# A stretch of products in a quantised feed-forward: twelve up units multiplied anew, down weights moved out of SBUF, gated units kept as magnitudes

## What is computed

```
def act_qdq(x):                      # 16 bits, one scale for the whole tensor
    scale = max(max(abs(x)) / 32767, 1e-12)
    return clip(round(x / scale), -32768, 32767) * scale

x    = act_qdq(layernorm(x1))
up   = act_qdq(x @ dequant(w_up).T)
gate = act_qdq(x @ dequant(w_gate).T)
sig  = clip(round(sigmoid(gate) * 65536), 0, 65535) / 65536
gate = act_qdq(gate * sig)
o    = act_qdq(gate * up)
out  = x1 + o @ dequant(w_down).T
```

## Time and profile before

| what | value |
|---|---|
| median of the runs | 2325.39 us |
| the profiled execution, whole / its span | 2322.58 us / 2320.7 us |
| mean granted TensorE clock | 0.948 |
| busy: PE, DVE, ACT, POOL | 88%, 72%, 60%, 25% |
| matmuls of gate and up stage | 620.83 to 1618.49 us |
| no matmul | 1618.49 to 1811.57 us |
| matmuls of the down stage | 1811.57 to 2307.9 us |

### The profile page before, as it was taken

One profiled execution on the slowest core, in us unless ns is written; L12 is line 12 of the kernel. 1 busy time (PEld: TensorE's weight loads), 2 busy tenths in 40 slices (PEclk: granted clock), 3 DMA queues, 4 the chain that ended last, 5 costly groups with the idle time before them and its releaser, 6 DMA issues.

```text
span 2320.7 us, 25770 instructions
## 1 busy us (share of the span) xinstructions
PE 2031.3 (88%) x9780; PEld 975.5 (42%) x9780; DVE 1678.2 (72%) x1385; ACT 1401.9 (60%) x1599; POOL 578.9 (25%) x600
## 2 busy tenths in 40 slices
PE   5899999998699999999999999998000799999998
PEld 2455555554344444444444444444000344444443
DVE  8799999999444443532699997999899644488641
ACT  4588888886322322322698995666899643467530
POOL 2587777776100000000112111222110000000000
PEclk9999999999799999999999999999555899999999
DMA  7689999997348647633899994787998755545641
GB/s 294 261 312 364 361 366 364 355 371 300 136 167 267 258 164 230 223 144 141 299 393 382 376 363 176 295 322 288 414 417 328 284 227 216 205 195 218 236 154 73
DMA packets 131163, 634.63 MB, mean 273 GB/s; under 512 B 12256, under 2 KB 12768, under 8 KB 91104
## 3 DMA queue, kind: packets, MB, share of 16 engines
q1 hardware_dynamic: 85888, 316.81, 37.3%
q0 software_dynamic: 45152, 316.16, 34.8%
HBM read 430.69 MB, written 202.24 MB: 273 GB/s over the span
## 4 chain that ended last, share of the span: by engine, by line
PE 64%; DVE 3%; issue 3%; ACT 2%; POOL 0%; DVEq 0%; ACTq 0%; POOLq 0%
PE fd_pp L1778 43%; PE fd_pp L1792 21%; ACT ff_ring L1721 1%; DVE ff_sig L1576 1%; DVE ff_h_parts L1560 1%; DVE ff_sq L1498 1%; ACT ff_sig L1708 0%; DVE ff_sq L1567 0%; DVE kept_gate L1569 0%; DVE ff_gin L1511 0%; DVE ff_hq L1550 0%; ACT ff_ring L1747 0%; ACT ff_sig L1737 0%; ACT ff_hq L1633 0%; DVE kept_o_peak L1576 0%
## 5 line engine op out<-in xcount | busy, mean ns | idle before, releaser
L1792 PE MATMUL fd_pp<-ff_down,kept_gate 128*128 128x512 f16 x1536 | 457.9, 380 | 193.1 <-DVE ff_up L1617 193.1
L1778 PE MATMUL fd_pp<-ff_h_parts,kept_gate 128*128 128x512 f16 x2304 | 500.4, 381 | 14.7 <-DVE ff_h_parts L1416 14.7
L1778 PE MATMUL fd_pp<-ff_h_parts,ff_up 128*128 128x512 f16 x2304 | 497.4, 379 | 0.0
L1640 ACT ACTIVATE ff_raw<-fd_pp 128x1024 f32<-128x1024 f32 x192 | 194.3, 1017 | 397.4 <-PE fd_pp L1778 397.4
L1778 PEld LDWEIGHTS fd_pp<-ff_h_parts,kept_gate 128*128 128x128 f16 x2304 | 226.1, 98 | 288.8 <-DVE ff_h_parts L1416 15.0
L1778 PEld LDWEIGHTS fd_pp<-ff_h_parts,ff_up 128*128 128x128 f16 x2304 | 225.4, 98 | 271.8
L1421 DVE TENSOR_REDUCE kept_gate_peak<-ff_raw 128x1 f32<-128x2048 f32 x48 | 109.7, 2285 | 293.5 <-ACT ff_raw L1640 293.5
L1792 PEld LDWEIGHTS fd_pp<-ff_down,kept_gate 128*128 128x128 f16 x1536 | 150.4, 98 | 375.2 <-issue 194.7
L1792 PE MATMUL fd_pp<-ff_down,ff_up 128*128 128x512 f16 x768 | 291.6, 380 | 0.0
L1747 ACT ACTIVATE ff_ring<-ff_hq,kept_g 128x2048 int16<-128x2048 f32 x48 | 96.0, 1999 | 189.5 <-DVE ff_hq L1550 188.2
L787 PE MATMUL at_psO<-kept_wo,at_ahi 128*128 128x512 f16 x512 | 154.9, 384 | 15.9 <-ACT at_alo L278 10.1
(11 more groups left out here) (239 smaller groups left out, 3311.8 us busy)
## 6 DMA issues: line engine op xcount, KB each, us to landing
ff_raw<-up_scratch SPq DMA_DIRECT2D x66, 1024.0 KB, 8.5
gate_scratch<-ff_raw POOLq DMA_DIRECT2D x48, 1024.0 KB, 9.1
ff_gin<-gate_scratch SPq DMA_DIRECT2D x48, 1024.0 KB, 8.4
up_scratch<-ff_raw POOLq DMA_DIRECT2D x48, 1024.0 KB, 6.8
ff_gin<-gate_integers SPq DMA_DIRECT2D x73, 512.0 KB, 6.3
gate_integers<-ff_ring POOLq DMA_DIRECT2D x43, 512.0 KB, 8.7
ff_up<-up_scratch SPq DMA_DIRECT2D x21, 1024.0 KB, 9.1
kept_xs<-in_x SPq DMA_DIRECT2D x32, 512.0 KB, 12.3
```

The lines of the kernel that those rows point to most:

```text
L1640: nc.scalar.activation(raw[:, n % UNITS, h * 2 * BLK:(h + 1) * 2 * BLK], pp[(2 * n + h) % 4][:, :, :].rearrange("p a t -> p (a t)"), ACT.C ...
L1778: mm = nc.tensor.matmul(pp[k % 4][:, h, :], wt[w][:, c, f:f + P], a[:, b % 2, :, c, :], start=(q == 0), stop=(q == len(todo) - 1))
L1792: mm = nc.tensor.matmul(pp[k % 8 // 2][:, k % 2, :], a[b % 2][:, f, t * P:(t + 1) * P], wt[w][:, f, :], start=(q == 0 and i == 0), stop=(q ...
```

## The change

The diff changes the constants, the order of the stretch, where up and down data lie, and what the gated units hold.

- READY goes from 36 to 40 and KEPT from 8 to 10. SECOND, worked out from READY, goes from 30 to 28, AGAIN = READY - KEPT from 28 to 30, late units from 12 to 8. The ring stays at 9 slots.
- In the second pass ACT takes the magnitude of every unit in place right behind its sigmoid, and DVE waits for it (`mag`) before its product. Only the 21 units that are loaded again in the stretch are stored, to a DRAM tensor of their own (`gated_magnitudes`); the gate integers stay in DRAM for the down stage.
- In the first pass all integers are made by ACT, one unit ahead; the separate magnitude `ab` goes, and DVE reduces the product with scale -1. The greatest positive gate value is found apart, by a second reduction per unit in the gate stage (`gate_top`).
- The up units of blocks 14, 13, 12 and 11 (12 of them, `anew`) are multiplied again by PE during the stretch, and ACT reads their magnitudes from PSUM in two halves. Two of these blocks' parts still lie in SBUF or are split at position 0; the splits of the other two stand at positions 11 and 22.
- The down weights (3 MB) are stored to DRAM late in the gate stage; their place becomes three load buffers of the stretch, and they are loaded back behind its last up loads. 33 up units are loaded, 29 gated ones.
- In the down stage every unit's gated integers are made again from the gate integers (before: 12 units).

The core of the diff:

```diff
-READY = 36
+READY = 40
-KEPT = 8
+KEPT = 10
...
+    anew = [b * UNITS + q for b in range(NB - 2, NB - 2 - BLOCKS, -1) for q in range(UNITS)]
+    anew_at = [UNITS + (7 * r + 1) // 2 for r in range(len(anew))]
...
+    order = list(range(NU - UNITS, NU)) + middle + list(range(UNITS))
+    for r, u in enumerate(anew):
+        order.insert(anew_at[r], u)
...
                 def load_hq(b):
-                    if b < NB:
+                    if b < NB + BLOCKS - 1:
...
-                        sp.dma_start(hq[:, b % 2, :], hq_d[b]).then_inc(hq_in[b % 2], 16)
+                        sp.dma_start(hq[:, b % 2, :], hq_d[block_of(NB + b)]).then_inc(hq_in[b % 2], 16)
...
+                    if n >= NU - 3:
+                        load_up(from_dram[n - (NU - 3)])
+                load_hq(NB + 1)
+                for i in from_dram[3:6]:
                     load_up(i)
+                load_hq(NB + 2)
+                for i in from_dram[6:]:
+                    load_up(i)
+                for j in range(3):
+                    sp.wait_ge(m["ua"], u_last["down", j] + 1)
+                    sp.dma_start(in_down[:, j, :], down_d[:, j, :]).then_inc(down_in[j], 16)
...
                 def store_gated(v):
-                    pool.wait_ge(m["g2"], v + 1)
-                    if v < KEPT:
-                        pool.dma_start(gate_q[AWAY + v], again(v)).then_inc(kept_out[v], 16)
-                    else:
-                        pool.dma_start(gate_q[v - KEPT], again(v)).then_inc(again_out[(v - KEPT) % AR], 16)
+                    if KEPT <= v < KEPT + LOADED:
+                        pool.wait_ge(m["g2"], v + 1)
+                        pool.dma_start(gate_m[v - KEPT], again(v)).then_inc(again_out[(v - KEPT) % AR], 16)
...
+                    if n < NU:
+                        nc.vector.tensor_reduce(keep["gate_top"][:, n:n + 1], raw[:, n % UNITS, :], AX.X, ALU.max)
...
                 def first(u):
                     sigmoid_integer(u, u % 2)
-                    gate_integers(u + 2)
-                    dve.wait_ge(m["ab"], u + 1)
...
-                def second(v):
-                    sigmoid_integer(NU + v, v % 2)
+                def second(v, a, t):
+                    sigmoid_integer(NU + v, a)
+                    dve.wait_ge(m["mag"], v + 1)
...
+                def last_gated(k):
+                    dve.wait_ge(m["fsig"], k + 1)
+                    need(dve, m["fgq"], k)
+                    nc.vector.tensor_scalar(sq[:, :], sig[:, k % 2, :], 65536.0, 65535.0, ALU.mult, ALU.min).then_inc(m["fsq"], 1)
...
                 for i in range(-2, NU):
                     k = i + 2
                     if k < NU and made[k] == "late":
...
+                        second(READY + nth(k), 0, gated(k))
+                    if i == 0:
+                        split(2 * NB)
+                    for b in range(1, BLOCKS - 1):
+                        if i == anew_at[UNITS * b - 1] + 1:
+                            split(2 * NB + b)
...
                 opk_v(dve)
+                last_gated(0)
                 last_product(0)
+                last_gated(1)
...
                     nc.scalar.activation(sig[:, k % 2, :], again(v), ACT.Sigmoid, scale=g[:, 4:5]).then_inc(m["sig"], 1)
-
-                def magnitude(v):
-
                     if v < KEPT:
                         act.wait_ge(kept_out[v], 16)
...
                     nc.scalar.activation(again(v), again(v), ACT.Abs).then_inc(m["mag"], 1)
...
+                        if order[i] in anew:
+                            k = 2 * NB * PAIRS + 2 * anew.index(order[i])
+                            for h in range(2):
+                                act.wait_ge(m["mm"], k + h + 1)
+                                nc.scalar.activation(ua[:, i % 3, h * 2 * BLK:(h + 1) * 2 * BLK],
...
+                for r, u in enumerate(anew):
+                    b, q = u // UNITS, u % UNITS
+                    pe.wait_ge(m["al"], 2 * NB + NB - 2 - b)
+                    for h in range(2):
+                        if r < 2:
+                            pe.wait_ge(m["out"], 2 * NB * PAIRS - 3 + 2 * r + h)
+                        elif h == 0:
+                            pe.wait_ge(m["ua_half"], r - 1)
+                        else:
+                            pe.wait_ge(m["ua"], anew_at[r - 2] + 1)
+                        two_rows(2 * NB * PAIRS + 2 * r + h, 2 * q + h, keep["up"], b % 2)
```

More of the change, by code:

```diff
@@ L944, in feed @@
     SECOND = NU - READY // 2
-    DONE = list(range(KEPT)) + [v for v in range(KEPT, READY) if v - KEPT >= AGAIN - AR][:5]
     LOADED = AGAIN - AR
-    WQ, NEAR = 4, 7
+    BLOCKS, NEAR = 4, 7
     FG, FU = 4, 3
@@ L951, in feed @@
     x1_v = x1_d.rearrange("(b n) p d -> b p n d", n=SUB)
[L953 to L965, removed]
-        else:
[L967 to L970, removed]
+    anew = [b * UNITS + q for b in range(NB - 2, NB - 2 - BLOCKS, -1) for q in range(UNITS)]
+    anew_at = [UNITS + (7 * r + 1) // 2 for r in range(len(anew))]
+    resident = [u for u in range(LOADED, AGAIN)]
+    fetched = [u for u in range(UNITS, LOADED)]
+    for n, u in enumerate(u for u in range(AGAIN, AWAY) if u not in anew):
+        fetched.insert(3 * n + 1, u)
+    middle = resident[:3]
+    for n, u in enumerate(fetched):
+        middle.append(u)
+        if n % 3 == 2:
+            middle += resident[3 + n // 3:4 + n // 3]
+    order = list(range(NU - UNITS, NU)) + middle + list(range(UNITS))
+    for r, u in enumerate(anew):
+        order.insert(anew_at[r], u)
+    made = ["late" if AGAIN <= u < AWAY else "ready" for u in order]
+    home = ["kept" if u >= AWAY else "ring" if LOADED <= u < AGAIN else "load" for u in order]
     def nth(i):
@@ L978, in at_home @@
         return home[:i].count(home[i])
-    from_dram = [i for i in range(NU) if order[i] < NU - UNITS]
+    from_dram = [i for i in range(NU) if order[i] < NU - UNITS and order[i] not in anew]
     place = {order[i]: i for i in range(NU)}
@@ L1083, in second_units @@
             return [v for v in range(READY) if SECOND + v // 2 == n]
-        def magnitude_at(n):
-            return [v for j, v in enumerate(DONE) if n == SECOND + max(3 + j if v < KEPT else 0, v // 2 + 2)]
         def kept(j):
-            return spare[:, j, :] if j < 6 else more[:, j - 6, :]
+            return spare[:, j, :] if j < 6 else more[:, j - 6, :] if j < 8 else ab[:, j - 8, :]
         def integers(u):
@@ L1106, in stored_first, with late_at @@
             return len(range(r, AWAY, QR))
+        def late_at(x):
+            return [i for i in range(NU) if made[i] == "late"][x]
         def have_gq(eng, u):
[L1110 to L1113, removed]
+            eng.wait_ge(m["gq"], u + 1)
         def gq_free(eng, u):
@@ L1131, in sq_free @@
                 need(eng, m["gpeak"], k)
-            elif k <= NU + READY:
+            else:
                 eng.wait_ge(m["g2"], k - NU)
[L1134 to L1138, removed]
         def gated(i):
-            kind, j = g_slot[i][0] if home[i] == "load" else ("unit", order[i])
-            if kind == "wq":
-                return hq[:, j, :] if j < 2 else ab[:, j - 2, :]
+            j = g_slot[i][0][1] if home[i] == "load" else order[i]
             return again(j - AWAY if j >= AWAY else j + KEPT)
@@ L1697, in _ @@
                     evict(NU + n, 1)
-                    for v in magnitude_at(n):
-                        magnitude(v)
                 AHEAD = 3
@@ L1750, in _, with two_rows @@
                         last_up(k)
[L1751 to L1762 removed]
+                    last_sigmoid(n + 6)
             @block.tensor
             def _(pe):
+                def two_rows(k, pair, wt, slot):
+                    for h in range(2):
+                        f = (2 * pair + h) * P
+                        todo = [(w, a, c) for c in range(DC) for w, a in ((0, ah), (0, al), (1, ah))]
+                        for q, (w, a, c) in enumerate(todo):
+                            mm = nc.tensor.matmul(pp[k % 4][:, h, :], wt[w][:, c, f:f + P], a[:, slot, :, c, :],
+                                                  start=(q == 0), stop=(q == len(todo) - 1))
+                    mm.then_inc(m["mm"], 1)
                 for b in range(2 * NB):
```

268 lines of the change are left out of this document (117 added, 151 removed).

## The result

| | before | changed kernel |
|---|---|---|
| median of the runs of that comparison | 2324.84 us (2323.17 to 2326.08, 4 runs) | 2345.56 us (2343.21 to 2347.48, 4 runs) |
| ratio, 95% interval | | 1.0089 (1.0072 to 1.0107) |
| the profiled execution, whole / its span | 2322.58 / 2320.7 us | 2346.77 / 2345.0 us |

The account below looks back on a forecast made before the run. The prediction took PE's two long matmul pieces, with the stretch between them, to bound the kernel. First product 29.6 us late, stretch 21 shorter and seam 6.6 longer gave 15.0 us over 2325.4: 2340.4, range 2320 to 2357.

Parts of the forecast that it names:

- The queue that is held: Up stage, second pass: block-integer loads stuck in SP's queue make four splits wait 9 us; first product 29.6 us late.
- Rival (b): Up stage: block loads land in DVE's slack, so the queue is not the bound; 2310.7 us, faster; chance 0.15.
- The even point: Up stage: chain from a peak's start to the split at which the change neither gains nor loses, 11 us; 14.8 forecast.
- Rival (c): Up stage: queue held, but transfers land near 3.8 us; first product 14.8 us late, 2325.6 us, no change; chance 0.13.
- The stretch: Stretch of products: DVE becomes the bound, 138.0 us of work plus 13 of waits; 151 us, 21 shorter.
- TensorE's part in the stretch: Stretch of products: PE's 12 units take 125 us and follow without setting the pace, if its clock stays at 1.00.
- rival (d): Chain 16.2 us, late loads 8.1, seam 19: 2357 us; also counts TensorE falling to clock 0.50 and staying; chance 0.12.
- The seam: Last product's end to PE's down-stage start: DVE's gated units ahead of o's scale make it 16.2 us, 6.6 more.
- The down stage is unchanged: Down stage: DVE goes from 274 to 401 of 488 us and PE still sets the pace, so no time added.
- The sum: Whole kernel: PE's down-stage start 15.0 us later, down stage unchanged; 2340.4 us against the median of 2325.4.

Follow-up runs that it names:

- e1: The changed kernel with SP's loads of the last five blocks' integers issued two loops earlier: 2313.07 us, ratio to before 0.9956.
- e2: The kernel before with SP's loads of the integers of blocks 12 to 15 issued one loop later: 2348.79 us, ratio 1.0108.
- e3: e1 with the gated loads of the stretch issued ten positions ahead in place of seven: 2305.60 us, ratio to before 0.9923.
- e7: The changed kernel with only the down stage's x loads issued three SP loops later: 2344.95 us, ratio to before 1.0096.
- e5: e3 with two of the seam's gated units made after o's scale and the down stage's x loads three SP loops later: 2300.40 us, ratio to before 0.9901.
- e6: e3 with the down stage's x loads issued three SP loops later, seam as in the changed kernel: 2305.69 us, ratio to before 0.9928.

## Why the prediction was right, and where not

**The queue that is held: right, in cause and size.** The splits wait 8.4 to 9.9 us where 9 was written, and end at 1491.9, 1531.9, 1570.7 and 1610.4 (each the next unit's start in DVE's timeline or the chain) where 1490.8, 1529.9, 1568.9 and 1608.0 were worked out; the first gate matmul already stood 2.6 us later. The first product is 29.2 us later behind that matmul, against 29.6. e1 takes this away and e2 puts it into the old kernel, so it is shown and not only argued. PE's waits are 17.8 us in three (5.5, 6.2, 6.1) where 20.7 was written (4.9 and twice 7.9); that does not enter the end, because the splits set the pace of DVE and so the last peak. What the prediction left out there is the clock. It gave PE 31.2 us for a block, but behind two of the waits a block takes 32.6 and 33.6 us (PE's timeline):

```profile
1532.03 32.56 PE L1747 MATMUL fd_pp<-ff_h_parts,ff_up 128*128 128x512 f16 x144 [5.48 <-DVE ff_h_parts L1399]
1570.83 33.63 PE L1747 MATMUL fd_pp<-ff_h_parts,ff_up 128*128 128x512 f16 x144 [6.23 <-DVE ff_h_parts L1399]
```

At their starts, and again at two starts in the stretch of products, the granted clock is 0.50 (stretches as above):

```profile
1531.40:1534.70 3.30, 2.67 (x7) 1.02 (x8) 3.27 (x3) 1.49 (x1) 0.00 (x0) 0.50 0.00 0
1569.00:1575.60 6.60, 4.78 (x12) 1.75 (x13) 6.53 (x5) 3.60 (x2) 0.00 (x0) 0.50 0.12 47
1681.60:1684.80 3.20, 2.55 (x7) 0.90 (x8) 3.16 (x4) 3.20 (x3) 0.00 (x0) 0.50 0.89 330
1777.20:1780.40 3.20, 2.54 (x7) 0.92 (x8) 3.20 (x5) 3.20 (x3) 1.06 (x2) 0.50 0.94 356
```

PE works 2.67 and 4.78 us at half the clock there, which loses 1.3 and 2.4 us and accounts for the longer blocks.

**Rival (b) is what the kernel would be without the hold**, 2310.7; e1 gives 2313.07. The even point of 11 us for the chain was not near: 14.2 at the first split. **Rival (c)** needed landings near 3.8 us; store and load took 4.3 to 6.9 us each in the chain.

**The stretch: gain right, its remainder mis-sized.** DVE's work of 138.0 us is measured at 138.7, and the stretch is 154.56 where 151 was written. The term that failed is the wait, put at 13 us, all of it for late loads; it measured 15.7. Of this 14.6 us are for late loads. The other 1.1 stand at position 17, ended by the magnitude of a unit from PSUM, and stand there as long in e3, so no load sets them. The landing was taken at 6.8 us; the five such loads on the chain of waits take 4.8 to 10.0 us, mean 7.9, where the DMA share is 0.88. The two long waits stand where they were worked out, three positions ahead of the late units at 9 and 35: 6.30 and 5.82 us where 4.3 was written for each, and the loads behind them landed in 9.1 and 8.6 us. By the same sum those landings make 6.6 and 6.1. The waits for the units at 15, 20 and 24, 3.8 us in all, did not come; 1.8 came for the unit at 28 and 0.6 for the one at 42, where 0 and 0.7 were written. Which units wait differs between executions of the same order: in e1 DVE stands 5.1 us at position 17, where ACT had waited for the load of the unit at 20. e3 shows that the loads' lead sets most of them: 7.9 us of the stretch come back with three positions more, and only the first stays.

The Trainium skill, page "HBM Reference", section "Specifications (TRN2)", says that a core streaming alone reaches about 425 GB/s, bounded by its 16 DMA engines. The trace agrees to about 1%: in slices of a fortieth of this stretch the changed kernel moves at most 430 GB/s, with the mean at 340.

**TensorE's part in the stretch: right, but for its clock.** It follows DVE and waits 17.0 us for PSUM halves. The prediction held that nothing shows a fall of the clock between matmuls so close; the rows above show it, at 0.50 from 1681.6 to 1684.8 and from 1777.2 to 1780.4 us, where PE had stood 5.4 and 6.1 us. But it did not stay there, as rival (d) counted: from 1700 to 1760 us its mean is 0.97. It stayed at 0.50 only when the last matmuls of the stretch were done (1800 to 1815 us). DVE set the pace throughout, so no time of the kernel is shown to hang on these falls.

**The seam: right**, 16.20 for 16.2. The rounding starts 10.7 us behind the last product's end (1815.96 to 1826.66), 10.5 was added up.

**"The down stage is unchanged": wrong, by 3.4 us.** The count of DVE's work was near (401 us written, 389.9 measured), and PE does set the pace. What the step left out is the same thing that the step on the up stage had found: what stands ahead of a load in SP's queue. It counted engines, and took the loads for hidden. As many loads stood behind the waits of `load_x` before (by the traces 43 such loads from 1811 us on, and 42 from 1830 us on after the change), but 36 of the 48 units now need theirs for a sigmoid, by the program two loops earlier. e7 gives 3.2 of the 3.4 us back. A smaller fault is the 496.34 us itself: that row of the chain covers 2292 matmuls of 2304, for the chain leaves PE ahead of its end. The last matmul of before stands in PE's timeline as

```profile
2310.11 0.38 PE L1792 MATMUL fd_pp<-ff_down,ff_up 128*128 128x512 f16 x1
```

which makes the stage 498.9 us. The expectations of e5, e6 and e7 inherited it: in the last two, 501.3 and 502.4 looked like 5 to 6 us of loss and were 2.4 and 3.4, which is why e6 and e7 gave less than was expected of them.

**The sum.** Predicted +15.0; the traces have +18.1 from the first gate matmul to the first down matmul (29.2 - 17.7 + 6.6), +3.4 in the down stage, and 2.6 ahead of the first gate matmul, where the change does nothing. The medians have +20.7. What was forecast wrong are thus two terms, 3.5 us of the stretch (17.7 gained for 21.2) and 3.4 of the down stage, both on the slow side; the late start of the profiled execution is no part of the mechanism.

## What to carry to other kernels

Where a queue is in order, look at what a load stands behind and not only at what it waits for: a constant that moves a ring's wait by one unit can hold a load that has nothing to do with the ring, and moving that load ahead is an edit of a few lines. Then check each other load of the same queue in the same way. An idle sum on an engine beside the bound says little of its price: read the waits of the engine that sets the pace, and measure a stage from first to last instruction, not by a row of the chain.

## What was not expected of the hardware

The first gate matmul stands at 618.89 us in one profiled execution (e5) and at 624.54 in another (e2), over kernels whose opening is the same: 5.65 us, more than the 0.2% that a comparison of medians was taken to resolve. Differences of 1 or 2 us can be sought only between two marks of the same trace behind that point, and not everywhere there: from the first gate matmul to the first product the changed kernel takes 1038.04 us and e7, which is the same up to there, 1040.29.

The granted clock fell to 0.50 at starts of PE behind waits of 5 to 6 us in a kernel whose mean clock is 0.975, and two blocks behind such waits in the up stage took 1.4 and 2.4 us longer than the 31.2 of before.
